# The product of B and C of a chunk as two products of 64 output rows

## The reference

```
proj = einsum('bld,pd->blp', xn, in_proj_w)          # gate, x, B, C, dt
xBC  = silu(conv(hbc))                                # causal, 4 taps, per channel
# 64 heads of 64 channels, 8 groups of 8 heads, B and C of 128 states per group
state = state * dA_t + dtx_t * B_t                    # step over the tokens
y_t   = einsum('bhpn,bhn->bhp', state, C_t)
y     = y + x * D;  yn = rmsnorm(y per group) * norm_weight * silu(gate)
out   = einsum('bli,di->bld', yn, out_proj_w)
```

## Time and profile before

| | |
|---|---|
| median of the runs | 2035.65 us |
| the profiled execution | 2041.41 us, span 2039.5 us |
| mean granted clock of TensorE | 0.983 of full |
| PE / PEld busy | 95% / 75% |
| DVE / ACT / POOL busy | 79% / 45% / 53% |
| line 1213 | 256 passes, 56.8 us of matmul, 39.0 us of weight load |

### The profile page before, as it was taken

The page is one execution under the profiler, slowest core; times in us unless marked ns, Lnnn a source line. Parts: engine busy times, 40 slices in busy tenths (PEclk is TensorE's granted clock), DMA queues, the critical chain, the costliest instruction groups (busy, mean ns, idle before and its releaser), DMA issues.

```text
span 2039.5 us, 27023 instructions
## 1 busy us (share of the span) xinstructions
PE 1928.8 (95%) x9624; PEld 1534.0 (75%) x9624; DVE 1617.7 (79%) x2000; ACT 924.0 (45%) x2070; POOL 1088.6 (53%) x888
## 2 busy tenths in 40 slices
PE   7978999999999999999898999999999999999997
PEld 5756877778787877877676787787878787787875
DVE  6878788787887877788786878878788787878784
ACT  4864453535445353544434445353443535354431
POOL 3136463654656464554555756365564646456465
PEclk9989999999999999999999999999999999999999
DMA  6222021121212112121233312112121201212113
GB/s 204 83 78 88 32 93 63 63 83 52 94 53 81 43 63 83 52 93 59 87 110 108 129 35 80 63 63 83 52 93 63 83 32 63 83 53 72 63 57 109
DMA packets 80534, 155.02 MB, mean 76 GB/s; under 512 B 8208, under 2 KB 27024, under 8 KB 80400
## 3 DMA queue, kind: packets, MB, share of 16 engines
q1 hardware_dynamic: 79360, 153.12, 22.4%
q10 hardware_dynamic: 1040, 0.17, 0.0%
HBM read 143.83 MB, written 9.44 MB: 75 GB/s over the span
## 4 chain that ended last, share of the span: by engine, by line
PE 56%; DVE 26%; ACT 9%; issue 6%; DMA 1%; POOL 1%; DVEq 0%; SPq 0%; POOLq 0%; ACTq 0%
DVE xc L710 7%; DVE decay L826 6%; PE ps_y L1203 6%; PE ps_conv L1047 5%; PE ps_conv L1050 5%; PE ps_gate L1047 4%; PE ps_gate L1050 4%; PE ps_out L1047 4%; PE ps_conv L1053 4%; PE ps_out L1050 4%; PE ps_y L1170 3%; PE ps_s L1165 3%; PE ps_gate L1053 3%; PE ps_out L1053 3%; DVE xw L838 2%
## 5 line engine op out<-in xcount | busy, mean ns | idle before, releaser
L710 DVE SCALAR_TENSOR_TENSOR xc<-ps_conv,convw_sb,xc 128x511 f32<-128x511 f32 (+2 forms) x576 | 430.2, 747 | 305.8 <-ACT xc L502 292.2
L1012 POOL TENSOR_TENSOR skip<-skip,y 128x512 f32<-128x512 f32 x112 | 358.1, 3197 | 47.3 <-DVE y L820 47.3
L826 DVE TENSOR_TENSOR_SCAN decay<-decay,eye 128x1024 f32<-128x1024 f32 x128 | 329.7, 2576 | 1.1 <-DMA decay<-decays_d 1.1
L992 POOL TENSOR_TENSOR skip<-x_tok,skip_bc 128x512 f32<-128x512 f32 x128 | 133.9, 1046 | 273.9 <-ACT x_tok L661 239.6
L1047 PE MATMUL ps_conv<-xn_hi,wconv_hi 128*128 128x512 f32 x768 | 247.9, 445 | 5.2 <-ACT xn_hi L555 4.1
L984 POOL TENSOR_TENSOR rstd_col<-mean_square,half 128x1 f32<-128x1 f32 x128 | 71.0, 554 | 330.1 <-ACT mean_square L640 330.1
L1203 PE MATMUL ps_y<-dtx,decay 128*128 128x128 f32 x1792 | 221.0, 275 | 0.3 <-DVE y L820 0.3
L508 ACT ACTIVATE xc<-xc 128x512 f32<-128x512 f32 x192 | 121.7, 634 | 219.1 <-DVE xc L710 219.1
L1203 PEld LDWEIGHTS ps_y<-dtx,decay 128*128 128x128 f32 x1792 | 211.5, 192 | 12.0 <-DVE y L820 0.5
L610 ACT ACTIVATE ynt_hi<-turned_y 128x512 fp32r<-128x512 f32 x128 | 76.4, 597 | 301.6 <-PE ps_out L1054 301.6
L1050 PE MATMUL ps_conv<-xn_hi,wconv_lo 128*128 128x512 f32 x768 | 208.6, 393 | 0.0
(11 more groups left out here) (196 smaller groups left out, 3933.2 us busy)
## 6 DMA issues: line engine op xcount, KB each, us to landing
decay<-decays_d SPq DMA_DIRECT2D x128, 512.0 KB, 4.5
stage<-w_in_t SPq DMA_DIRECT2D x32, 1024.0 KB, 5.2
stage<-w_out_t SPq DMA_DIRECT2D x16, 1024.0 KB, 5.3
stage<-w_in_t SPq DMA_DIRECT2D x32, 256.0 KB, 3.3
out_sum<-hidden SPq DMA_DIRECT2D x16, 256.0 KB, 4.4
next_x<-hidden SPq DMA_DIRECT2D x16, 256.0 KB, 3.7
io<-ffn_d SPq DMA_DIRECT2D x16, 256.0 KB, 2.8
out<-out_sum SPq DMA_DIRECT2D x16, 256.0 KB, 2.0
```

The costliest lines, as they stand in the source:

```text
L710: e.scalar_tensor_tensor(acc[:, d:], ps[:, 0:BLK - d], convw_sb[:, tile, TAPS - 1 - d:TAPS - d], acc[:, d:], ALU.mult, ALU.add).then_inc(S ...
L826: e.tensor_tensor_scan(d[:, :], d[:, :], eye8[:, :, :].rearrange("p h i -> p (h i)"), 0.0, ALU.mult, ALU.add).then_inc(S["scan"], 1)
L992: e.tensor_tensor(by_head(skip[i % 2][:, :]), by_head(x_tok[:, :]), heads_bc(skip_bc[:, gi * GH:(gi + 1) * GH]), ALU.mult).then_inc(S["ski ...
L1012: e.tensor_tensor(skip[m % 2][:, :], skip[m % 2][:, :], y[m % 2][:, :], ALU.add).then_inc(S["base"], 1)
```

## The change

In place of one product of 128 output rows there are two of 64: the stationary operand is cut into its first and its last 64 columns, the moving operand is the same, and the results go to the first and the last 64 partitions of the same 128 columns of `ps_s`. HD is 64, P is 128. Each product is issued for the part of the array whose columns match its output's partitions. The semaphore rises with the second one. All waits stay.

```diff
-                    e.matmul(ps_s[:, 0:P], xb[:, XT, cc], xb[:, XT + 1, cc], start=True, stop=True).then_inc(S["mm_g"], 1)
+                    bs = xb[:, XT, cc]
+                    e.matmul(ps_s[0:HD, 0:P], bs[:, 0:HD], xb[:, XT + 1, cc], start=True, stop=True)
+                    e.matmul(ps_s[HD:P, 0:P], bs[:, HD:P], xb[:, XT + 1, cc], start=True,
+                             stop=True).then_inc(S["mm_g"], 1)
```

## The result

The changed kernel takes 2070.86 us (2069.78 to 2071.95) against 2035.65 before: 35 us longer, a ratio of 1.0167 with a 95% interval from 1.0151 to 1.0184. The forecast was 2084 in a range from 2047 to 2104.

The account below looks back on a forecast made before the run. TensorE was taken to bound the kernel at 79 of 128 chunks, VectorE and ScalarE deciding the others. 79 x 0.66 = +52 us, -4 for the clock, gave +48 on 2035.65: about 2084 us, range 2047 to 2104.

Parts of the forecast that it names:

- Slower, and where: Whole kernel: slower, about 2084 us; added TensorE time counts where TensorE decides, not in the stretch VectorE and ScalarE decide.
- The count of 79: Chain of waits: the changed product of line 1213 stands on it 79 times of 128, so added time counts 79 times.
- Passes in series, +0.223 us: Changed product on TensorE: four passes in series at 0.112 us, 0.446 for 0.223 now, +0.223 us per chunk.
- overlap in a rival: Half products: second's first pass beside first's second, three pass times for four; chance 0.14 with switches, 0.08 with free switch.
- Emptying at each switch, +0.435: Before and after the half products: array must be empty at each partition change, 0.165 going in, 0.27 coming out.
- its sign of being wrong: Timeline at the changed product: prediction is wrong if the first half's load still starts under line 1205; no size.
- Per chunk 0.66, on the path 52 us: Changed product: 0.223 for passes plus 0.435 for emptying, 0.66 us per chunk; 79 times on the chain, +52 us.
- the 0.67 forecast: Fourth chunk, line 1165: TensorE's wait of 2.15 us takes up the delay and shrinks to about 0.67 us.
- The clock, -4: Fourth chunk's steps: with the wait shorter some low-clock steps may go, between 0 and -8 us, -4 taken.
- The rivals with a free switch: Partition change costs nothing: products in series, 2053 us, chance 0.22; or halves overlapping, 2032 to 2040 us, chance 0.08.
- uncovered loads: Half products: each half pass waits for its own load, about 1.0 us per chunk, +84, about 2120 us; chance 0.09.
- the one with overlap and switches at 2075: Half products overlap, with an empty array at each switch: 0.55 us per chunk, +39, 2075 us; chance 0.14.

## Why the prediction was right or wrong

*Slower, and where: right.* The added time of TensorE counts in the fifth to eighth and the first chunk of a group, and VectorE's and ScalarE's stretch swallowed the rest. The count of 79 was somewhat high: 18.9 us are 70 times 0.27. The first group's chunks carry it too, but the group with the second sequence's normalisation carries 0.3 us in all beside its one step at the low clock, and the ninth group half.

*Passes in series, +0.223 us: wrong.* Four passes take 0.05 us less than two did, so this term is -0.05. The prediction allowed overlap in a rival, but for one pair of passes only, "the order of issue allows no more". The timeline after shows both pairs side by side, and one half left out changes nothing. The Trainium skill (TensorE: Matmul & The Clock Gate, section on measured speedup and the span model) counts a few ns for each further column tile; the 0.007 us between the two halves' starts agree with that. One reading behind the term does not hold either: that the streamed columns alone set the 0.112 us. Line 1205's two passes with 64 columns start 0.06 us apart, but in the trace before, its loads and the next product's follow each other every 0.112 us (905.82, 905.93, 906.04), as those of line 1203 do (the row below is line 1205's two loads in the kernel before). Loads of 128 columns come as far apart as streams of 128, so the whole product of line 1205 gains nothing by streaming 64. In the heads cut in halves loads and streams both became shorter; neither was shortened alone.

```profile
905.82 0.30 PEld L1205 LDWEIGHTS ps_y<-dtx,decay 128*128 128x128 f32 x2
```

*Emptying at each switch, +0.435: right in kind, too large.* The gaps add 0.15 and 0.19 us, 0.34 together. The prediction priced them by the modelled ends of the records, 0.275 us after a pass starts; the next load came 0.20 us after it. By the letter, its sign of being wrong even shows: the first half's load, at 1405.69, starts 0.07 us before the modelled end of line 1205's last record (1405.76), though 0.15 us later than before. That a change of mode drains TensorE (the Trainium skill, TensorEngine Tiling, section Tiling Modes) is borne out by the halves set apart: some 0.3 of the 0.54 us more are two further changes.

*Per chunk 0.66, on the path 52 us: 0.27 and 19.* This is the term that was mis-sized, by both steps above. So TensorE's wait in the fourth chunk fell to 1.86 us and not to the 0.67 forecast.

*The clock, -4: wrong in sign.* It is +12 (in the two profiled executions) to +16. The step took it that a shorter wait (2.15 us, now 1.86) would be answered less often by the low clock. It is answered more often here, in 11 groups for 5, and never at 1.61. That the low clock needs the wait is shown by the filling; why the same wait, at 2.15 or at 1.86 us, drops the clock in some groups and not in others is not settled, and so it stays open why the change made it more frequent. The whole product issued twice, with a wait of 1.9 us and no change of the partition, has 6 long steps; whether the array's emptying before the wait adds some was not tested by itself. With the same steps the number of long ones differs between kernels (11 regular ones after the change, 7 with one half, 10 with quarters), and one kernel's runs spread by up to 10 us (one half, 2062 to 2072.5).

The two misses, 33 us too much for the chunks and some 16 to 20 too little for the clock, cancelled by more than half. That the total came within 13 us is luck: of the mechanism forecast, the emptying array happened, and the passes in series and the clock's relief did not. The rivals with a free switch and with uncovered loads are excluded; the nearest was the one with overlap and switches at 2075, with the switch too dear and the overlap too small.

## What to carry to other kernels

Count the changes of the array's partition, not the half products: each pair of changes, in and out, cost TensorE about 0.3 us here, so put all the products that can go in halves next to each other, the two halves alternating, and look for a gain where 64 streamed columns had been padded to 128. Before pricing a few tenths of a microsecond per step, look at the granted clock of the steps: a wait of TensorE of some 2 us can cost another 1.6 us behind it, and filling it can give that back (5.5 us in the kernel before, 20 in the changed one).

## What the runs showed of the hardware that was not expected

- Passes of float32 half products overtake each other: first and second pass of both halves start in pairs, 0.007 us apart, and eight passes of four quarters take what four passes take (0.36 us from load to load).
- The overtaking reaches a few passes, not sixteen: with the heads' halves eight products apart, each side's passes ran one behind the other at 0.06 us but for the tail.
- Half products with 64 streamed columns run at 0.06 us per pair of passes, against 0.112 per pass of a whole one, whose loads of 128 columns follow each other at 0.112 us whether 128 or 64 columns are streamed.
- More work for TensorE can make the kernel faster: eight products of 512 columns that nobody reads, put into its wait, took the kernel before to 0.9972 of its time (0.9962 to 0.9983) and the changed one from 2070.9 to 2050.7 us, because the clock stayed up.
